# Ranks read as marked minima, and a third target one-hot of eight on ScalarE, in a graph convolution on one core

## The chip, the cores and the metric

One Trainium2 chip, one of its cores. The metric is the device time of one execution of the program in microseconds (us). The kernel before takes 6993.59 us, the median of 3 runs (6985.06 to 7000.94).

## What is computed

Two graph convolutions over 25,000 nodes and 250,000 edges, then a lookup of 102,400 rows. Cut to what matters:

```python
def gcn_conv(x, W, b, row, col, num_nodes):
    h = x @ W
    row_sl, col_sl = [row, loop], [col, loop]          # every node also has an edge to itself
    deg = segment_sum(ones, col_sl); dinv = rsqrt(max(deg, 1))
    msg = h[row_sl] * (dinv[row_sl] * dinv[col_sl])[:, None]
    return segment_sum(msg, col_sl) + b
h1 = gcn_conv(emb, W1, b1, row, col, 25000)            # 64 -> 128 features
lookup = gcn_conv(h1, W2, b2, row, col, 25000)         # 128 -> 64 features
return lookup[r_input]                                 # 512 x 200 rows of 64
```

The kernel multiplies the two weight matrices first, so both rounds of messages carry 64 features.

## The kernel before

**Stages.** (1) A histogram of the targets' blocks and degrees. (2) A counting sort of the edges by target block of 256 nodes (98 blocks), in 5 chunks of 50,000 edges; a chunk is 50 *sort batches* of 8 columns of 125 edges. (3) Round 1 of the messages: for each chunk, GpSimd gathers the source rows from a table in HBM (`L371`, 392 indirect DMAs of 128 rows per chunk, 1960 per round), and *visits* add them up: a visit makes a one-hot of the targets (128x256), multiplies it on TensorE with the 128 gathered rows (`L656`), and VectorE adds the product to the block's accumulator (`L1037`). A chunk has 61 *visit batches* of 8 visits. (4) Round 2 does the 5 chunks' visits again on the rescaled table. (5) GpSimd fetches the asked rows with 800 indirect DMAs (`L404`) and SyncE writes them out.

**The sort batch.** For batch `s`, VectorE makes block one-hots (`block_onehots`, 125x784: 8 edge columns by 98 blocks). TensorE adds to the running ranks in PSUM (`rank_ps`, 98 ranks for each of 8 columns) how many edges of lower partitions go to each block (`rank_before`, 2 matmuls of 392 columns with the triangle `before`). Then VectorE reads each edge's rank: `pick_ranks` (`L988`) multiplies ranks by one-hots, `sum_ranks` (`L994`) sums over the blocks. `rank_rest` on TensorE (2 matmuls with `not_before`) adds the rest of the batch's counts, once `pick_ranks` has read. `cut_places` splits the rank into a partition and a column, `cast_places` and `partition_onehots` turn the partition into one-hots, and `column_onehot` (`L1016`, 8 per batch, 125x488) makes the column one-hots. ScalarE scales the partition one-hots by two digits of the edge (`scale_column`, `L457`, 16 per batch), and TensorE places them (`place_column`, 16 matmuls of 488 columns).

**How the stages lie over each other.** Chunk 0 is sorted first, together with the multiplication of the embeddings by the weights (`sort_batch`, batches 0 to 48 with 4 embedding matmuls `L709` and VectorE's scaling `L1124` inside). After chunk 0's `decode` the gathers start, 6 more sort batches run (`AHEAD`), and then `both` runs one sort batch of the next chunk beside one visit batch of this one: 50 such batches for chunks 0 to 2, 44 for chunk 3, whose other 11 or 17 visit batches run alone. Chunk 4 of round 1 and all of round 2 have no sort beside them. VectorE's instructions in `both` are in the order of the list `BOTH`; TensorE's in the order of its own `both`: `rank_before(s + 1)`, then for each `k` visit `k` and column `k`, with `rank_rest(s + 1)` after `k == 0`.

**Who makes the target one-hots.** In chunks 0 to 3 of round 1, `ON_ACT = (3, 6)` names the two of eight that ScalarE makes, each by two activations (`L464`, the distance, and `L468`, one minus it); VectorE makes the other six (`L1027`). In `both`, ScalarE makes one before its 16 scalings and the other after the fourth column's. From chunk 4 of round 1 on VectorE makes all eight.

**The gathers' ring.** Gathered rows lie in a ring of 16 gather batches of 8. A gather batch may start once the visit batch is multiplied that could still use its place:

```python
if c * GB + b >= RINGB:
    c0, b0 = divmod(c * GB + b - RINGB, GB)
    done = (r * CHUNKS + c0) * VB + min(b0 + LAG, VB - 1) + 1
    pool.wait_ge(visits_multiplied, done * W8 + VISIT_CREDIT)
```

With `GB` = 49 gather batches, `VB` = 61 visit batches and `LAG` = 13, gather batch 16 of a chunk waits for visit batch 13 of the same chunk, and batches 0 to 15 for visit batches 46 to 60 of the chunk before. The gathers of a chunk also wait for its `sources_ready`, which `copy_tiles` raises during the chunk before. TensorE waits for landed rows in `wait_landed`, behind `rank_before` and ahead of the batch's first visit.

## Time and profile before

| what | value |
|---|---|
| median of 3 runs | 6993.59 us |
| the profiled execution: its own time, its span | 6975.57 us, 6973.8 us |
| granted clock of TensorE, mean | 0.692 |
| busy of the span: PE, DVE, ACT, POOL | 72%, 61%, 30%, 65% |
| gathers of both rounds (L371) | 3920, busy 3785.5 us |
| fetches of the asked rows (L404) | 800, busy 754.7 us |

The profiled execution is 18 us below the median of the runs. Busy shares are means over stages with different limits, so the stages have to be read apart; "idle before, releaser" says what an engine's idle time ended with. In the rows, PE is TensorE's matmul, PEld its weight load, DVE VectorE, ACT ScalarE, POOL GpSimd.

### The profile page before, as it was taken

Reading aid. Unit: us, or ns where it says so; the run is one execution under the profiler, and the core shown is the slowest. Engines: PE = TensorE matmul, PEld = TensorE weight load, DVE = VectorE, ACT = ScalarE, POOL = GpSimd, SP = SyncE. Lnnn points to the kernel's source line nnn. Section 1 sums busy time; section 2 is a strip of 40 time slices with the busy share of each in tenths; the row PEclk is TensorE's granted clock in tenths of the full one; section 3 lists DMA queues with packets and bytes.
Section 4 is the critical chain, followed back from the end, with each engine's and each line's share of the span. In section 5 each row is a group of like instructions: output and inputs, shape, how many; then the busy total and the mean of one; then the engine's idle time right before and its main releaser. Section 6 shows DMA issues by size and latency. Waiting matters only on the chain.

```text
span 6973.8 us, 133704 instructions
## 1 busy us (share of the span) xinstructions
PE 5035.2 (72%) x27034; PEld 4251.7 (61%) x27035; DVE 4284.9 (61%) x14137; ACT 2098.6 (30%) x6145; POOL 4543.0 (65%) x4733
## 2 busy tenths in 40 slices
PE   6858788888888888899788888888888888100000
PEld 5633355755655665799788888888888888100000
DVE  8988899899889889767566555555555555000000
ACT  7957666566566566511100000000000011000000
POOL 0000377767767767777677777777777777677777
PEclk9989999899899999855555555555555555555555
DMA  0001111111111111111111111111111111111111
GB/s 14 0 18 39 27 25 25 27 21 25 26 21 25 26 20 25 26 36 41 37 26 26 26 26 26 26 26 26 26 26 26 34 39 39 45 53 53 53 53 52
DMA packets 184476, 210.96 MB, mean 30 GB/s; under 512 B 81356, under 2 KB 100182, under 8 KB 184336
## 3 DMA queue, kind: packets, MB, share of 16 engines
q0 software_dynamic: 151040, 154.97, 11.3%
q1 hardware_dynamic: 15280, 35.45, 1.3%
q10 hardware_dynamic: 18016, 19.05, 0.9%
q8 instruction: 42, 0.69, 0.0%
q14 instruction: 98, 0.80, 0.0%
HBM read 163.62 MB, written 45.54 MB: 30 GB/s over the span
## 4 chain that ended last, share of the span: by engine, by line
PE 34%; POOL 25%; issue 19%; DVE 14%; DMA 6%; DVEq 3%; ACT 0%; POOLq 0%; SPq 0%; ACTq 0%
PE ps L656 24%; POOL scratch L371 14%; POOL acc L404 11%; PE ps L561 9%; DMA scratch<-table,source 5%; DVE late L1016 3%; DVE place_i L994 3%; DVE acc L1037 2%; DVE hi_onehot L829 2%; DVE late L1027 1%; DVE picked L988 1%; PE ps L709 1%; DVE prt_onehot L829 0%; DVEq L1035 0%; DVEq L1027 0%
## 5 line engine op out<-in xcount | busy, mean ns | idle before, releaser
L371 POOL DMA_INDIRECT scratch<-table,source x3920 | 3785.5, 966 | 2154.1 <-issue 1104.5
L656 PEld LDWEIGHTS ps<-scratch,late 128*128 128x128 f32 x19520 | 3685.6, 283 | 766.2 <-issue 643.7
L656 PE MATMUL ps<-scratch,late 128*128 x19520 | 3723.5, 368 | 455.6 <-SPq L336 259.6
L1037 DVE TENSOR_TENSOR acc<-acc,ps 128x128 f32 x4880 | 1357.8, 278 | 1250.9 <-PE ps L656 1225.9
L1027 DVE TENSOR_SCALAR late<-ramp,target 128x256 f32<-128x256 f16 x4392 | 1654.2, 377 | 162.1 <-issue 95.0
L457 ACT ACTIVATE late<-prt_onehot,scratch 125x128 f16<-125x128 f16 x4000 | 1214.7, 387 | 699.6 <-DVE prt_onehot L829 600.0
L561 PE MATMUL ps<-late 125*128 125x488 f16 x4000 | 1125.1, 372 | 164.6 <-DVE late L1016 164.5
L404 POOL DMA_INDIRECT acc<-lookup,scratch x800 | 754.7, 943 | 267.4 <-issue 243.5
L533 ACT ACTIVATE acc<-acc,dinv (+1 forms) x196 | 57.5, 340 | 2441.9 <-DVE acc L1037 2441.9
L1016 DVE TENSOR_SCALAR late<-ramp,tcol 125x488 f16<-125x488 f16 x2000 | 685.0, 350 | 0.0
L561 PEld LDWEIGHTS ps<-late 125*128 125x128 f16 x4000 | 363.7, 113 | 314.7 <-DVE late L1016 203.7
L561 PE MATMUL ps<-scratch,hi_onehot 125*98 125x265 f16 x2000 | 283.2, 283 | 67.8 <-DVE hi_onehot L829 51.3
L438 ACT ACTIVATE scratch<-ramp,acc 125x257 f16<-125x257 f16 x750 | 317.7, 501 | 27.1 <-DVE scratch L838 16.3
L468 ACT ACTIVATE late<-distance,one_col 128x256 f32<-128x256 f16 x488 | 247.8, 508 | 258.1 <-PE ps L656 216.5
L988 DVE TENSOR_TENSOR picked<-ps,blk_onehot 125x784 f32<-125x784 f32 x250 | 243.6, 975 | 132.9 <-PE ps L561 132.1
L561 PEld LDWEIGHTS ps<-scratch,hi_onehot 125*98 125x98 f16 x2000 | 215.8, 125 | 135.3 <-DVE hi_onehot L829 131.0
L464 ACT ACTIVATE distance<-ramp,target 128x256 f16<-128x256 f16 x488 | 241.8, 496 | 3.6
L994 DVE TENSOR_REDUCE place_i<-picked 125x8 int32<-125x784 f32 x250 | 239.5, 958 | 0.0
L829 DVE TENSOR_TENSOR scratch<-ramp,acc 125x1280 f16<-125x1280 f16 x250 | 206.0, 824 | 17.9 <-PE ps L561 5.1
L533 ACT ACTIVATE acc<-acc,dtmp (+1 forms) x196 | 57.5, 340 | 407.5 <-DVE acc L1037 407.5
L561 PE MATMUL ps<-blk_onehot,not_before 125*128 125x392 f16 x500 | 128.0, 338 | 71.3 <-DVE picked L988 67.1
L561 PE MATMUL ps<-blk_onehot,before 125*128 125x392 f16 x500 | 126.8, 336 | 64.0 <-issue 53.7
(145 smaller groups left out, 1079.1 us busy)
## 6 DMA issues: line engine op xcount, KB each, us to landing
scratch<-table,source POOLq DMA_INDIRECT x3920, 2.5
out<-acc SPq DMA_DIRECT2D x40, 640.0 KB, 3.0
acc<-lookup,scratch POOLq DMA_INDIRECT x800, 2.4
table<-acc SPq DMA_DIRECT2D x49, 128.0 KB, 2.5
table<-acc ACTq DMA_DIRECT2D x49, 128.0 KB
lookup<-acc ACTq DMA_DIRECT2D x49, 128.0 KB
late<-embT ACTq DMA_DIRECT2D x47, 128.0 KB, 2.7
scratch<-edge_index SPq DMA_DIRECT2D x2, 976.6 KB
```

The costliest lines, as they stand in the source:

```text
L371: pool.indirect_dma_start(out=place, out_offset=None, in_=table[r], in_offset=bass.IndirectOffsetOnAxis(ap=source[:, t:t + 1], axis=0)).th ...
L404: pool.indirect_dma_start(out=out_rows[:, h, k, :], out_offset=None, in_=lookup, in_offset=bass.IndirectOffsetOnAxis(ap=ask_i[:, t:t + 1], ...
L438: act.activation(lo_rows[0:EP, b, j, 0:LOW + 1], ramp[0:EP, 0:LOW + 1], ACT.Sign, bias=lo_half[0:EP, bass.ds((i * 2 + b) * W8 + (c * CB * ...
L457: act.activation(piece[0:EP, k, j, :], prt_onehot[0:EP, b, j, :], ACT.Copy, scale=digit[k][0:EP, bass.ds(s * W8 + j, 1)]).then_inc(pieces_ ...
L561: return pe.matmul(dst, lhsT, rhs, start=False, stop=False, skip_group_check=True)
L656: last = pe.matmul(visit_ps[odd * W8 + k][:, n * FEAT:(n + 1) * FEAT], target_onehot[:, odd * W8 + k, n * P:(n + 1) * P], row, start=True, ...
L829: return dve.tensor_tensor(place.rearrange("p j (w r) -> p j w r", r=2), of_row.rearrange("p (w r) -> p w r", r=2).unsqueeze(1).broadcast_ ...
L988: dve.tensor_tensor(picked[E, :, :].rearrange("p (h j) n -> p h (j n)", h=2), rank_ps[E, :, :], blk_onehot[E, :, :].rearrange("p (h j) n - ...
L994: dve.tensor_reduce(place_i[E, 0, :], picked[E, :, :], AX.X, ALU.add).then_inc(rank_step, 1)
L1016: dve.tensor_scalar(tcol_onehot[E, j % TRING, :], ramp[E, 0:CV], tcol[E, b, j:j + 1], None, ALU.is_equal).then_inc(tcol_onehots, 1)
L1027: dve.tensor_scalar(target_onehot[:, odd * W8 + k, :], ramp[:, 0:BN], target[:, bass.ds((g - r * BATCHES) * W8 + k, 1)], None, ALU.is_equa ...
L1037: dve.tensor_tensor(dst, dst, visit_ps[odd * W8 + k].rearrange("p (n f) -> p n f", f=FEAT), ALU.add).then_inc(visits_added, 1)
```

## The change

`pick_ranks` and `sum_ranks` become one instruction, `least_ranks`. The triangle `before` carries -65536 on its diagonal, so after `rank_before` the rank of the block that an edge goes to is by far the least of its 98, and a minimum over the blocks, read straight from PSUM, gives it. The mark is a multiple of 128 and 512, so cutting out partition and column drops it. `rank_rest` takes it away again: `after` carries +65536 on the diagonal, and a second matrix, `itself`, adds the edge's own 1, so `rank_rest` is 4 matmuls, not 2. The matrices and the block one-hots are BF16. `rank_rest` stands later in TensorE's order (after column 1 in the sort alone, after column 2 in `both`). ScalarE makes the one-hots 2, 5 and 7. GpSimd makes three more small matrices at the start.

```diff
-ON_ACT = (3, 6)
+ON_ACT = (2, 5, 7)
...
-        blk_onehot = sb("blk_onehot", [P, W8, NB], F16)
-        picked = sb("picked", [P, W8, NB], F32)
+        blk_onehot = sb("blk_onehot", [P, W8, NB], BF16)
...
-            pool.affine_select(out=not_before[:, :], in_=ones[:, :], compare_op=ALU.is_ge, fill=0.0,
+            pool.affine_select(out=after[:, :], in_=ones[:, :], compare_op=ALU.is_gt, fill=0.0,
                                base=0, pattern=[[-1, P]], channel_multiplier=1).then_inc(triangles_made, 1)
+            pool.affine_select(out=itself[:, :], in_=ones[:, :], compare_op=ALU.is_equal, fill=0.0,
+                               base=0, pattern=[[1, P]], channel_multiplier=-1).then_inc(triangles_made, 1)
+            pool.wait_ge(triangles_made, 3)
+            for triangle, mark in ((before, -MARK), (after, MARK)):
+                pool.affine_select(out=triangle[:, :], in_=triangle[:, :], compare_op=ALU.not_equal, fill=float(mark),
+                                   base=0, pattern=[[1, P]], channel_multiplier=-1).then_inc(triangles_made, 1)
...
                     scale_column(s, j, b)
-                    if j == 3 and between is not None:
-                        act_onehot(between, ON_ACT[1], odd)
+                    if between is not None and j in (2, 5):
+                        act_onehot(between, ON_ACT[1 + j // 5], odd)
...
                 pe.wait_ge(rank_step, s * RANK + 1)
-                for h in range(2):
-                    last = add(rank_ps[:, h, :], not_before[0:EP, :], halves[0:EP, h, :])
+                for counted_by in (after, itself):
+                    for h in range(2):
+                        last = add(rank_ps[:, h, :], counted_by[0:EP, :], halves[0:EP, h, :])
                 last.then_inc(rank_advanced, 1)
...
                 place_column(s, 0)
+                place_column(s, 1)
                 rank_rest(s + 1)
-                place_column(s, 1)
                 pe.wait_ge(emb_loaded[b], i * 16 + 16)
...
-                    if more and k == 0:
+                    if more and k == 2:
                         rank_rest(s + 1)
...
-            def pick_ranks(s):
+            def least_ranks(s):
+
                 dve.wait_ge(rank_summed, s + 1)
-                dve.tensor_tensor(picked[E, :, :].rearrange("p (h j) n -> p h (j n)", h=2), rank_ps[E, :, :],
-                                  blk_onehot[E, :, :].rearrange("p (h j) n -> p h (j n)", h=2), ALU.mult).then_inc(rank_step, 1)
-
-            def sum_ranks(s):
-                dve.wait_ge(rank_step, s * RANK + 1)
-                with nc.allow_low_precision(reason="one whole number among zeros"):
-                    dve.tensor_reduce(place_i[E, 0, :], picked[E, :, :], AX.X,
-                                      ALU.add).then_inc(rank_step, 1)
+                with nc.allow_low_precision(reason="a whole number"):
+                    dve.tensor_reduce(place_i[E, 0, :].rearrange("p (h j) -> p h j", h=2),
+                                      rank_ps[E, :, :].rearrange("p h (j n) -> p h j n", n=NB), AX.X,
+                                      ALU.min).then_inc(rank_step, 1)
...
-BOTH = [("blocks",), ("target", 0), ("column", 0), ("late add", 4), ("target", 1), ("pick",), ("late add", 5), ("column", 1),
-        ("target", 2), ("sum",), ("late add", 6), ("column", 2), ("cut",), ("late add", 7), ("column", 3), ("load",),
-        ("target", 4), ("add", 0), ("cast",), ("column", 4), ("target", 5), ("add", 1), ("partitions",), ("column", 5),
-        ("add", 2), ("column", 6), ("target", 7), ("add", 3), ("column", 7)]
+BOTH = [("blocks",), ("target", 0), ("column", 0), ("late add", 4), ("target", 1), ("late add", 5), ("column", 1),
+        ("target", 3), ("least",), ("late add", 6), ("column", 2), ("cut",), ("late add", 7), ("column", 3), ("load",),
+        ("target", 4), ("add", 0), ("cast",), ("column", 4), ("target", 6), ("add", 1), ("partitions",), ("column", 5),
+        ("add", 2), ("column", 6), ("add", 3), ("column", 7)]
```

How the order moves, at the places that the prediction speaks of. First VectorE in `both`, the first half of a batch, from the block one-hots on (`tcol` are the column one-hots, `target` the target one-hots, `picked` and the reduction the two steps of reading the ranks; the adds are not in the part of the loop shown, whose first batch has none). Before:

```order
L829 TENSOR_TENSOR blk_onehot<-ramp,scratch 125x784
L1027 TENSOR_SCALAR late<-ramp,target 128x256
L1016 TENSOR_SCALAR late<-ramp,tcol 125x488
L1027 TENSOR_SCALAR late<-ramp,target 128x256
L988 TENSOR_TENSOR picked<-ps,blk_onehot 125x784
L1016 TENSOR_SCALAR late<-ramp,tcol 125x488
L1027 TENSOR_SCALAR late<-ramp,target 128x256
L994 TENSOR_REDUCE place_i<-picked 125x8
L1016 TENSOR_SCALAR late<-ramp,tcol 125x488
L1000 TENSOR_SCALAR place_i<-place_i 125x8
```

Of the change:

```order
L840 TENSOR_TENSOR blk_onehot<-ramp,scratch 125x784
L1036 TENSOR_SCALAR late<-ramp,target 128x256
L1025 TENSOR_SCALAR late<-ramp,tcol 125x488
L1036 TENSOR_SCALAR late<-ramp,target 128x256
L1025 TENSOR_SCALAR late<-ramp,tcol 125x488
L1036 TENSOR_SCALAR late<-ramp,target 128x256
L1001 TENSOR_REDUCE place_i<-ps 125x8
L1025 TENSOR_SCALAR late<-ramp,tcol 125x488
L1008 TENSOR_SCALAR place_i<-place_i 125x8
L1009 TENSOR_SCALAR tcol<-place_i 125x8
```

`L988` is gone, the reduction (now `L1001`) reads `ps`, and it stands one column and one target one-hot later behind the block one-hots.

TensorE in `sort_batch`, from `rank_before` to the embedding matmuls (`late` are the pieces that are placed; `L618` and `L628` hold the wait for the ranks' reading). Before:

```order
L561 MATMUL ps<-blk_onehot,before 128x392 x2
L624 ISA
L625 ISA
L561 MATMUL ps<-late 128x488 x2
L618 ISA
L561 MATMUL ps<-blk_onehot,not_before 128x392 x2
L624 REGISTER_ALU
L625 REGISTER_ALU
L561 MATMUL ps<-late 128x488 x2
L709 MATMUL ps<-w,late 128x64 x4
```

Of the change:

```order
L571 MATMUL ps<-blk_onehot,before 128x392 x2
L635 ISA
L636 ISA
L571 MATMUL ps<-late 128x488 x2
L635 REGISTER_ALU
L636 REGISTER_ALU
L571 MATMUL ps<-late 128x488 x2
L628 ISA
L571 MATMUL ps<-blk_onehot,after 128x392 x2
L571 MATMUL ps<-blk_onehot,itself 128x392 x2
L720 MATMUL ps<-w,late 128x64 x4
```

Column 1's two matmuls moved ahead of the wait, and behind it stand four rank matmuls, directly ahead of the embedding matmuls.

TensorE in `both`, around `rank_rest` (`scratch,late` is a visit). Before:

```order
L656 MATMUL ps<-scratch,late 128x64 x2
L624 ISA
L625 ISA
L561 MATMUL ps<-late 128x488 x2
L618 ISA
L561 MATMUL ps<-blk_onehot,not_before 128x392 x2
L649 REGISTER_ALU
L653 ISA
L656 MATMUL ps<-scratch,late 128x64 x2
```

Of the change:

```order
L667 MATMUL ps<-scratch,late 128x64 x2
L635 REGISTER_ALU
L636 REGISTER_ALU
L571 MATMUL ps<-late 128x488 x2
L628 ISA
L571 MATMUL ps<-blk_onehot,after 128x392 x2
L571 MATMUL ps<-blk_onehot,itself 128x392 x2
L660 REGISTER_ALU
L664 ISA
L667 MATMUL ps<-scratch,late 128x64 x2
```

`rank_rest` now follows the third column and not the first, and has four matmuls.

## Rows read from the trace of the kernel before

**Rows 1.** The page: POOL's busy share and TensorE's granted clock in 40 slices.

```profile
POOL 0000377767767767777677777777777777677777
PEclk9989999899899999855555555555555555555555
```

**Rows 2.** Busy time by stretch: stretch, length, PE, PEld, DVE, ACT, POOL, clock, DMA.

```profile
1513.00:2058.00 545.00, 469.79 (x2960) 335.78 (x2960) 483.21 (x1615) 351.84 (x1044) 390.57 (x391) 0.96 0.13 24
...
3104.00:3440.00 336.00, 310.76 (x1447) 308.93 (x1447) 223.19 (x863) 42.26 (x144) 251.87 (x266) 0.50 0.18 40
3466.00:5950.00 2484.00, 2106.67 (x9715) 2082.32 (x9715) 1351.63 (x5061) 55.16 (x188) 1853.99 (x1960) 0.50 0.15 28
5967.00:6973.00 1006.00, 0.00 (x0) 0.00 (x0) 0.00 (x0) 0.00 (x0) 754.73 (x800) 0.50 0.16 52
```

**Rows 3.** Waits from 831 to 2990 us (us, times, longest), and one in POOL's timeline.

```profile
POOL scratch L371 <- PE ps L656: 118.7, 75, 34.2
...
1505.78 0.94 POOL L371 DMA_INDIRECT scratch<-table,source  x1 [30.11 <-PE ps L656]
```

**Rows 4.** Timeline of DVE, one batch of both: start, us, what, idle before.

```profile
1609.72 0.55 DVE L829 TENSOR_TENSOR blk_onehot<-ramp,scratch 125x784 f16<-125x784 f16 x1
1610.20 0.34 DVE L1027 TENSOR_SCALAR late<-ramp,target 128x256 f32<-128x256 f16 x1
1610.46 0.34 DVE L1016 TENSOR_SCALAR late<-ramp,tcol 125x488 f16<-125x488 f16 x1
...
1611.47 0.97 DVE L988 TENSOR_TENSOR picked<-ps,blk_onehot 125x784 f32<-125x784 f32 x1 [0.21 <-PE ps L561]
1612.36 0.28 DVE L1037 TENSOR_TENSOR acc<-acc,ps 128x128 f32 x1
...
1613.15 0.95 DVE L994 TENSOR_REDUCE place_i<-picked 125x8 int32<-125x784 f32 x1
...
1619.17 0.55 DVE L829 TENSOR_TENSOR blk_onehot<-ramp,scratch 125x784 f16<-125x784 f16 x1
```

**Rows 5.** Timeline of PE in the same batch: ranks, visits, a column, visits.

```profile
1612.50 0.51 PE L561 MATMUL ps<-blk_onehot,not_before 125*128 125x392 f16 x2 [0.17 <-DVE picked L988]
1612.84 0.56 PE L656 MATMUL ps<-scratch,late 128*128 x4
1613.24 0.58 PE L561 MATMUL ps<-late 125*128 125x488 f16 x2
1613.65 0.55 PE L656 MATMUL ps<-scratch,late 128*128 x4
```

**Rows 6.** Timeline of ACT in the same batch.

```profile
1611.75 2.43 ACT L457 ACTIVATE late<-prt_onehot,scratch 125x128 f16<-125x128 f16 x8
1614.09 0.50 ACT L464 ACTIVATE distance<-ramp,target 128x256 f16<-128x256 f16 x1
1614.70 0.51 ACT L468 ACTIVATE late<-distance,one_col 128x256 f32<-128x256 f16 x1
1617.83 1.57 ACT L457 ACTIVATE late<-prt_onehot,scratch 125x128 f16<-125x128 f16 x5 [2.62 <-DVE prt_onehot L829]
```

**Rows 7.** Timeline of PE, then of DVE, in one batch of the sort alone.

```profile
611.80 0.51 PE L561 MATMUL ps<-blk_onehot,not_before 125*128 125x392 f16 x2 [0.66 <-DVE picked L988]
...
607.24 0.42 DVE L1124 TENSOR_TENSOR acc<-ps,dinv 128x256 f32 x1 [0.32 <-PE ps L709]
...
610.77 0.97 DVE L988 TENSOR_TENSOR picked<-ps,blk_onehot 125x784 f32<-125x784 f32 x1 [0.75 <-PE ps L561]
...
613.93 0.42 DVE L1124 TENSOR_TENSOR acc<-ps,dinv 128x256 f32 x1 [0.32 <-PE ps L709]
```

**Rows 8.** Timeline of POOL: a gather beside DVE's partition one-hots (1607.48 to 1608.16).

```profile
1607.56 1.42 POOL L371 DMA_INDIRECT scratch<-table,source  x1 [0.30 <-issue]
```

**Rows 9.** A stretch at the granted clock of 0.50, and a column pair in it.

```profile
434.00:442.00 8.00, 4.25 (x11) 1.06 (x12) 5.95 (x13) 2.52 (x9) 0.00 (x0) 0.50 0.08 5
...
440.61 1.02 PE L561 MATMUL ps<-late 125*128 125x488 f16 x2
```

More of the change, by code:

```diff
@@ L120, in build @@
         ones = sb("ones", [P, P], F16)
-        before = sb("before", [P, P], F16)
-        not_before = sb("not_before", [P, P], F16)
+        before = sb("before", [P, P], BF16)
+        after = sb("after", [P, P], BF16)
+        itself = sb("itself", [P, P], BF16)
         hi_onehot = sb("hi_onehot", [P, 2, W8, NT], F16)
@@ L1101, in first_places @@
                 block_onehots(s)
-                pick_ranks(s)
-                sum_ranks(s)
+                least_ranks(s)
                 cut_places(s, 0)
@@ L1168, in both @@
                         block_onehots(s + 1)
-                    elif what == "pick":
-                        pick_ranks(s + 1)
-                    elif what == "sum":
-                        sum_ranks(s + 1)
+                    elif what == "least":
+                        least_ranks(s + 1)
                     elif what == "cut":
```

29 lines of the change are left out of this document (15 added, 14 removed).

## The prediction, made before the changed kernel was run

> **What bounds the kernel now.** I read the page's 40 slices first [rows 1]: POOL has the same seven or eight tenths in nearly every slice from 793 us to the end, while PE, DVE and ACT change from stage to stage. So the gathers may set the end, and the question for each stage is whether POOL works back to back. The table of stretches answers it [rows 2]. In round 2 1960 gathers take 2484 us, 1.267 us each. In the last 266 gathers of round 1 they come every 336 / 266 = 1.263 us. The same pace in both: POOL is the bound there, with PE at the lower clock level (0.50 granted) and still not in the way. The fetches of the asked rows, 800 in 1006 us, are also one after another. Nothing of the change touches these stages.
>
> In chunks 1 to 3 of round 1, where sort and visits run together, POOL makes 391 gathers in 545 us, 1.394 us each [rows 2]. Its waits show why: 118.7 us of them end with a visit on TensorE. Most of the 75 are the usual 0.3 us between two gathers, but once per chunk, in chunks 1 to 3, POOL stands still for 30 to 34 us [rows 3]. This is the ring's wait of gather batch 16 for visit batch 13 of the same chunk. Without it the chunk's gathers would take 545 - 31 = 514 us (1.315 us each, a little over round 2's pace). So the period of a chunk is set by the sort and visit batches, but **only by 31 us**; behind them stands POOL.
>
> What sets those batches is VectorE. From one block one-hot to the next it takes 1619.17 - 1609.72 = 9.45 us [rows 4], and idles only 0.21 us ahead of `pick_ranks` and shortly at the register load. ScalarE waits 2.62 us for the partition one-hots [rows 6].
>
> Before the gathers there are 49 sort batches with embeddings, 613.93 - 607.24 = 6.69 us each [rows 7].
>
> **The change, part by part.**
>
> *The first gather.* It starts when chunk 0 is sorted, so the sort alone is on the path, and a reading by busy time would promise 49 x 0.97 us for the lost `pick_ranks`. The timeline says otherwise [rows 7]: VectorE's embedding scaling waits 0.32 us for TensorE's embedding matmuls, and these stand behind `rank_rest`, which waits for `pick_ranks` to end. The new minimum starts where `pick_ranks` started (behind `rank_before`, which VectorE already awaits for 0.75 us, time enough for one more column one-hot), so if it lasts as long, `rank_rest` is released at the same moment. It then has two matmuls more, and one column pair fewer ahead of the embedding matmuls. A rank pair costs 1612.84 - 1612.50 = 0.34 us, a column pair 1613.65 - 1613.24 = 0.41 us [rows 5]. The batch gets 0.41 - 0.34 = 0.07 us shorter, and VectorE waits about 1.2 us for the embedding matmuls instead of 0.32. That is 49 x 0.07 = 3.4 us, say **-4 us** with the one batch without embeddings. The minimum's duration is unknown: nearest are the reduction over as many elements from SBUF (0.95 us) and the product that reads the same ranks from PSUM (0.97 us) [rows 4]. I take 0.97; a reduction that costs the two together, 1.92, is the other end, and one at half the product's time, 0.5, the lower.
>
> *A batch of `both` on VectorE.* Gone are `pick_ranks` with its slot, 1612.36 - 1611.47 = 0.89 us, the wait ahead of it, 0.21 us, which two more instructions now cover, and one target one-hot, 1610.46 - 1610.20 = 0.26 us [rows 4]. 9.45 - 1.36 = **8.1 us**.
>
> *The same batch on TensorE.* At the full clock a visit and a column pair take 1613.65 - 1612.84 = 0.81 us [rows 5]. 8 x 0.81 + 2 rank matmuls before and now 4 after, 3 x 0.34 = 1.0 us, makes 7.5 us, under 8.1. In its new place `rank_rest` finds the minimum done, because column 2, ahead of it, is made behind the minimum on VectorE.
>
> *The same batch on ScalarE.* 8 scalings take 1614.09 - 1611.75 = 2.34 us, a one-hot's first step 0.61 us and its second 0.51 at most. 2 x 2.34 + 3 x 1.12 = 8.0 us [rows 6], also under 8.1, but near: three engines now lie within 0.6 us. The third one-hot's 1.12 us is hidden in the 2.62 us that ScalarE waits; where that cover is gone it is on the path. I allow 8.4 us for the batch in all.
>
> *The chunk.* 50 batches that are 9.45 - 8.4 = 1.05 us or more shorter bring the chunk's own work from 545 to 492 us or less. POOL needs 514. So the ring's wait vanishes, POOL works without a pause, TensorE waits instead for landed rows, and **the period becomes POOL's 514 us**. The gain is the waits and no more: 118.7 less 75 x 0.3 = **-96 us** [rows 3]. It stands for any batch under 9.45 - 31 / 50 = 8.83 us: most of what the change saves on VectorE (50 x 1.36 = 68 us a chunk) lands in a wait.
>
> *At no cost:* three more small matrices on GpSimd, which has no other work before the first gather at 793 us; BF16 for F16, two bytes either way; the mask in `cut_places`, inside an instruction that is there anyway.
>
> *Sum:* -4 - 96 = -100 us. The profiled execution took 6975.6 us, so 6875.6 by its measure; the median of the runs is 18 us above it, so **6893.6 us**. A measurement of this kernel tells 0.2%, 14 us, from no change.
>
> **The rivals.**
>
> *The batch shrinks too little* (chance 0.15). The minimum costs the two old steps together, or the three near-equal engines wait for each other. At 9.1 us a batch the chunk's work is 545 - 17.5 = 527 us, the ring's wait is still 13 us of 31, and three chunks give some 55 us with the start's gain: 6939 us. For it: VectorE, TensorE and ScalarE at 8.1, 7.5 and 8.0. Against it: the bound to clear is 8.83.
>
> *The gathers slow down* (0.05). A gather beside the partition one-hots took 1.42 instead of 0.94 us [rows 8]. If a denser VectorE meets one such in every batch where now it meets fewer, up to 50 x 0.48 = 24 us a chunk are added to 514, and the end is within 20 us of today's, 6985 us. Against it: the number of these instructions per gather does not grow.
>
> *The clock falls* (0.05, the slower side). TensorE gets a new wait inside `both`, for landed rows, ahead of each batch's first visit. The granted clock in chunks 1 to 3 is now 0.96, that is mostly the 2.4 GHz level; in the visits without a sort beside them it is 0.50, 1.2 GHz, with PE 85% to 92% busy [rows 2]. If the waits bring the lower level into `both`, columns cost 0.82 us a pair instead of 0.41 (1.02 us for a pair from first start to last end, against 0.58) and ranks double likewise [rows 5, 9]; a visit costs at most 336 us / 1447 x 4 = 0.93 us, against 0.40 [rows 2, 5]. The batch is then 8 x 1.75 + 2 = 16 us, 7.6 us over the 8.4 allowed. The decisive point is (545 - 492) / 7.6 = 7 batches of 50: beyond it a chunk is longer than today. With one in four, 12, it is 492 + 91 = 583 us, 38 more than today for each of four chunks: 7145 us, or some 7070 us if the lone visits catch up half of it. Against it: a batch of 8.4 to 8.8 us holds the same matmuls as one of 9.45, so PE is denser, not thinner. The Trainium skill (TensorE: Matmul & The Clock Gate, The HAM clock gate) says that recent activity releases the throttle and that waits inside the loop bring it back; by that rule the new wait would argue for this rival, while the denser batch argues against.
>
> *More is gained* (0.09). Either the sort alone does shorten by VectorE's 0.97 us, 49 x 0.97 = 48 us instead of 4, or POOL's pace in `both` comes down to round 2's 1.267 us, 391 x 0.048 = 19 us a chunk: 6820 to 6850 us. The Trainium skill (SBUF — State Buffer, Who interferes with whom) says that GpSimd shares a port pair with VectorE, that `tensor_scalar` in its faster modes takes the pair for its whole duration and that `tensor_reduce` never does; by that rule a target one-hot fewer on VectorE helps the gathers. One of 14 such instructions in a batch is worth 19 / 14 = 1.4 us a chunk by the rows, so I leave it out of the sum.
>
> *The batch does not shrink at all*, because ScalarE's late one-hots hold TensorE (0.02): 6990 us.
>
> **How the numbers follow.** The forecast has 0.64. With the first rival and the larger gain, faster by over 0.2% has 0.64 + 0.15 + 0.09 = 0.88; the slower gathers and the batch that doesn't shrink make 0.07 for within 0.2%; the clock makes 0.05 for slower. The range runs from 6855, the forecast with a part of the larger gain, to 6950, the first rival with 10 us of scatter of the runs. It leaves out the three cases at the top and most of the larger gain.
>
> **What would show it.** Right: the three waits of 30 us on POOL are gone, and 391 gathers take 510 to 520 us; the wait of PE for SyncE's count of landings, which in round 1's chunks does not occur now, appears; blocks of one-hots come every 8.1 to 8.8 us; VectorE's wait for the embedding matmuls grows to about 1.2 us while the batch stays near 6.6 us; the first gather starts 3 to 6 us earlier; the reduction from PSUM takes about 0.97 us. Wrong: waits of POOL for visits that remain (the batch is over 8.83 us), a granted clock well under 0.95 in chunks 1 to 3, or a first gather tens of us earlier.

## The result, and the profile after

The changed kernel takes **6868.89 us** (6868.16 to 6871.3, 4 runs), the kernel before in the same comparison 6996.85 us (6985.06 to 7000.94, 4 runs): ratio 0.982, 95% interval 0.9803 to 0.9837. That is 128 us less; the forecast was 100 less, 6893.6 us. The profiled executions took 6975.57 and 6869.0 us, 106.6 us apart.

The page of the changed kernel, busy time and the slices of POOL and of TensorE's granted clock, against [rows 1]:

```profile
span 6867.3 us, 134775 instructions
PE 5034.4 (73%) x27534; PEld 4382.0 (64%) x27535; DVE 4014.0 (58%) x13643; ACT 2327.5 (34%) x6633; POOL 4539.2 (66%) x4736
...
POOL 0000377777777777777677777777777777677777
PEclk9989999899899899555555555555555555555555
```

POOL's sixes in slices 9, 12 and 15, the starts of chunks 1 to 3, are gone; the two left, slices 20 and 35, are the steps from round 1 to round 2 and from round 2 to the fetches, and stand in the kernel before too.

Busy time by stretch of the changed kernel, columns as in [rows 2]: chunk 2, the last 272 gathers of round 1, round 2, the fetches:

```profile
1447.00:1960.00 513.00, 472.06 (x3077) 374.77 (x3076) 426.73 (x1513) 409.32 (x1169) 386.99 (x392) 0.90 0.13 26
2990.00:3333.00 343.00, 292.75 (x1351) 289.27 (x1351) 206.55 (x801) 39.91 (x136) 257.01 (x272) 0.50 0.18 39
3360.00:5843.00 2483.00, 2106.56 (x9714) 2082.23 (x9714) 1349.76 (x5061) 55.15 (x188) 1854.11 (x1960) 0.50 0.15 28
5860.00:6867.00 1007.00, 0.00 (x0) 0.00 (x0) 0.00 (x0) 0.00 (x0) 755.05 (x800) 0.50 0.17 52
```

Only the first row has changed: 392 gathers in 513 us, where 391 took 545. ScalarE's busy time there rose from 352 to 409 us, VectorE's fell from 483 to 427. The clock fell from 0.96 to 0.90.

Waits of the changed kernel from 700 to 2900 us (total, times, longest), against [rows 3], and at the end POOL's own row from 700 to 3500 us (in a row, `a <- b` is a waiting for b):

```profile
DVE acc L1046 <- PE ps L667: 133.8, 70, 5.7
ACT late L467 <- DVE prt_onehot L840: 100.5, 87, 15.3
...
PE ps L667 <- SPq L340: 72.9, 33, 4.2
...
POOL scratch L381 <- PE ps L667: 23.5, 77, 0.3
```

POOL's waits for a visit are down to 77 of 0.3 us; the three of 30 us are gone. New is TensorE's wait for SyncE's count of landings, 72.9 us in 33 pieces: TensorE is now ahead of the rows.

VectorE and TensorE in the sort alone, one batch of the changed kernel, against [rows 7]:

```profile
606.83 0.97 DVE L1001 TENSOR_REDUCE place_i<-ps 125x8 int32<-125x784 f32 x1 [0.49 <-PE ps L571]
...
607.87 0.51 PE L571 MATMUL ps<-blk_onehot,after 125*128 125x392 bf16 x2 [0.25 <-DVE place_i L1001]
...
608.21 0.49 PE L571 MATMUL ps<-blk_onehot,itself 125*128 125x392 bf16 x2
...
608.63 1.10 PE L720 MATMUL ps<-w,late 64*128 64x64 f32 x8
...
609.92 0.42 DVE L1131 TENSOR_TENSOR acc<-ps,dinv 128x256 f32 x1 [1.38 <-PE ps L720]
...
613.45 0.97 DVE L1001 TENSOR_REDUCE place_i<-ps 125x8 int32<-125x784 f32 x1 [0.48 <-PE ps L571]
```

The minimum from PSUM takes 0.97 us. The batch takes 613.45 - 606.83 = 6.62 us, where it took 6.69: what VectorE saved now stands in its wait for the embedding matmuls, 1.38 us instead of 0.32.

**Where the 106 us of the trace come from.** POOL's time up to the last gather of round 1 can be closed as a sum: start of the first gather, plus what its waits for a visit exceed the usual 0.3 us each ("excess"), plus what the 1960 gathers last beyond 0.944 us each ("lengthening"; 0.944 us is their median), plus a rest. For every kernel of the table the rest is 2471 to 2475 us, so these three columns explain the difference between any two to within 4 us. (Added up from the records of each trace, one execution each, us; the kernels below the second are the experiments. The medians come from three groups of runs, so they compare to some 13 us: the kernel before had 6996.9, 6984.9 and 6983.7 in the three.)

| kernel | first gather | excess | lengthening | last gather of round 1 | median of runs |
|---|---|---|---|---|---|
| before | 793.2 | 96.2 | 81.2 | 3442.7 | 6996.9 |
| changed | 786.6 | 0.4 | 76.1 | 3336.4 | 6868.9 |
| ranks alone | 787.8 | 0.3 | 112.6 | 3371.6 | 6901.0 |
| third one-hot alone | 794.2 | 69.1 | 72.9 | 3408.0 | 6960.2 |
| changed + two minima | 788.0 | 166.4 | 53.4 | 3482.4 | 7031.7 |
| changed + a one-hot | 787.6 | 0.4 | 58.6 | 3317.8 | 6849.0 |
| changed + a short minimum | 788.1 | 0.3 | 56.0 | 3317.2 | 6845.2 |
| changed, embedding first | 734.5 | 0.4 | 77.0 | 3283.7 | 6815.9 |
| before, embedding first | 789.1 | 112.0 | 77.8 | 3451.1 | 6986.1 |

From before to changed: -6.6, -95.8, -5.1, and 1.2 in the rest. Nine tenths of the gain are the waits.

### The profile page after: what moved, and what is told of

The parts are those of the page before. It is cut to its first block, busy times and chain, and to the rows that moved or that the text cites. A ratio compares the mean times of both kernels' runs of the same rounds, so it can differ in the third digit from the quotient of the medians.

```text
span 6867.3 us, 134775 instructions
## 1 busy us (share of the span) xinstructions
PE 5034.4 (73%) x27534; PEld 4382.0 (64%) x27535; DVE 4014.0 (58%) x13643; ACT 2327.5 (34%) x6633; POOL 4539.2 (66%) x4736
## 4 chain that ended last, share of the span: by engine, by line
PE 36%; POOL 30%; issue 17%; DVE 7%; DMA 7%; DVEq 2%; ACT 0%; POOLq 0%; SPq 0%; ACTq 0%
PE ps L667 25%; POOL scratch L381 19%; POOL acc L414 11%; PE ps L571 10%; DMA scratch<-table,source 7%; DVE hi_onehot L840 2%; DVE acc L1046 1%; DVE place_i L1001 1%; DVE late L1025 1%; PE ps L720 1%; DVE late L1036 1%; DVE scratch L840 0%; DVEq L1044 0%; DVEq L854 0%; DVE prt_onehot L840 0%
## 5 line engine op out<-in xcount | busy, mean ns | idle before, releaser
L667 PEld LDWEIGHTS ps<-scratch,late 128*128 128x128 f32 x19520 | 3751.6, 286 | 822.4 <-issue 657.5
L1036 DVE TENSOR_SCALAR late<-ramp,target 128x256 f32<-128x256 f16 x4148 | 1564.2, 377 | 149.0 <-issue 71.5
L467 ACT ACTIVATE late<-prt_onehot,scratch 125x128 f16<-125x128 f16 x4000 | 1236.4, 387 | 306.3 <-DVE prt_onehot L840 151.2
L571 PEld LDWEIGHTS ps<-late 125*128 125x128 f16 x4000 | 397.6, 119 | 146.2 <-DVE late L1025 60.8
L478 ACT ACTIVATE late<-distance,one_col 128x256 f32<-128x256 f16 x732 | 371.8, 508 | 263.9 <-PE ps L667 199.6
L474 ACT ACTIVATE distance<-ramp,target 128x256 f16<-128x256 f16 x732 | 362.9, 496 | 5.2
L448 ACT ACTIVATE scratch<-ramp,acc 125x257 f16<-125x257 f16 x750 | 318.5, 501 | 26.4 <-DVE scratch L849 16.3
L1001 DVE TENSOR_REDUCE place_i<-ps 125x8 int32<-125x784 f32 x250 | 241.6, 967 | 67.5 <-PE ps L571 67.2
L840 DVE TENSOR_TENSOR prt_onehot<-ramp,prt 125x1024 f16<-125x1024 f16 x250 | 170.1, 681 | 0.3
L840 DVE TENSOR_TENSOR blk_onehot<-ramp,scratch 125x784 bf16<-125x784 f16 x250 | 140.0, 560 | 10.3 <-issue 9.8
L571 PE MATMUL ps<-blk_onehot,before 125*128 125x392 bf16 x500 | 126.6, 335 | 25.1 <-issue 19.0
```

Of the source, the lines that this page charges most:

```text
L448: act.activation(lo_rows[0:EP, b, j, 0:LOW + 1], ramp[0:EP, 0:LOW + 1], ACT.Sign, bias=lo_half[0:EP, bass.ds((i * 2 + b) * W8 + (c * CB * ...
L467: act.activation(piece[0:EP, k, j, :], prt_onehot[0:EP, b, j, :], ACT.Copy, scale=digit[k][0:EP, bass.ds(s * W8 + j, 1)]).then_inc(pieces_ ...
L474: act.activation(distance[:, 0:BN], ramp[:, 0:BN], ACT.Abs, bias=target[:, bass.ds(g * W8 + k, 1)], scale=-1.0).then_inc(distances, 1)
L478: act.activation(target_onehot[:, odd * W8 + k, :], distance[:, 0:BN], ACT.Relu, bias=one_col[:, 0:1], scale=-1.0).then_inc(act_onehots, 1)
L571: return pe.matmul(dst, lhsT, rhs, start=False, stop=False, skip_group_check=True)
L667: last = pe.matmul(visit_ps[odd * W8 + k][:, n * FEAT:(n + 1) * FEAT], target_onehot[:, odd * W8 + k, n * P:(n + 1) * P], row, start=True, ...
```

## Experiments

My theory: POOL's own pace is a floor of 514 us a chunk, VectorE's batch sets the time only above 8.83 us, and in the sort alone the order on TensorE, not VectorE's work, sets the batch. The rivals: each us of VectorE counts wherever it is; it was ScalarE's one-hots or the clock; POOL's pace itself changes. (The *knee* below is the 8.83 us at which, by the prediction, VectorE's batch takes over from POOL.)

### First group: four kernels on a chip that behaves otherwise

*Ranks alone*: the changed kernel with two of eight on ScalarE again. *Third alone*: the kernel before, with three.

```diff
 # ranks alone, against the changed kernel
-ON_ACT = (2, 5, 7)
+ON_ACT = (3, 6)
 # third alone, against the kernel before: the same line the other way
```

(The conditions at ScalarE's columns and the target entries of the `BOTH` table follow it.) *Least twice* and *least thrice*: one or two spare minima into an unused tile, in every batch of `both`:

```diff
                 dve.wait_ge(rank_summed, s + 1)
+                for k in range(again):
...
+                        dve.tensor_reduce(spare_i[E, k, :]..., rank_ps[E, :, :]..., AX.X, ALU.min)
```

> The marked minimum without the third one-hot on ScalarE. Theory (round 1's chunks end with GpSimd's 514 us once a batch of both is under 8.83 us): VectorE's batch is 8.1 + 0.26 = 8.4 us, still under 8.83, so no wait of POOL for a visit over 1 us, and the time is the changed kernel's within 0.2%, 6869 us plus or minus 14. Rival (each part gives its share of VectorE's time, 1.1 and 0.26 us of 1.36): a fifth of the 106 us is missing, 6890 us.

> The kernel before with ScalarE making one-hots 2, 5 and 7. Theory: VectorE's batch is 9.45 - 0.26 = 9.2 us, over 8.83, so the long waits of POOL stay but shrink by 50 x 0.26 = 13 us each to some 18 us; three of them give 40 us, about 6955 us; the first gather stays at 793 us. Rival (ScalarE is in the way): no change, 6997 us.

> The changed kernel, with a second minimum of the same ranks, into a spare tile, in each batch of both. Theory: a batch is 8.1 + 0.89 = 9.0 us, just over the knee of 8.83; a chunk's own work is 545 - 50 x 0.47 = 521 us against POOL's 514, so waits of about 7 us are back once per chunk and the time is some 20 us above the changed kernel's, 6890 us. Rival (VectorE bounds round 1): 194 x 0.89 = 173 us slower, 7040 us.

> As before it with two spare minima in each batch of both. Theory: a batch is 9.9 us, past the knee each further microsecond counts: 50 x 0.89 = 44 us per chunk over the run with one spare minimum, in the three waits 134 us more, about 7025 us, and POOL waits of some 50 us. Rival (slack is left elsewhere): under 60 us more than the run with one spare minimum.

Measured: 9192.61, 9270.21, 9200.81 and 9243.82 us, where the kernel before took **9261.68 us** (9229 to 9283, 19 runs) on this chip. Ratios 0.9927 [0.9906, 0.9948], 1.0011 [1.0002, 1.0021], 0.9933 [0.9911, 0.9955], 0.9984 [0.9971, 0.9996]. The changed kernel itself was not run there. None of the expectations could be judged: another bound stood over them. The third one-hot alone ran later on an ordinary chip too, so one kernel's stretches (the sort alone, a chunk of `both`, round 2) can be set side by side. On this chip:

```profile
440.00:740.00 300.00, 244.47 (x1237) 119.27 (x1238) 250.23 (x709) 214.81 (x716) 0.00 (x0) 0.98 0.14 39
1878.00:2651.00 773.00, 550.69 (x2971) 409.67 (x2970) 475.65 (x1561) 412.82 (x1167) 387.47 (x392) 0.80 0.09 17
4680.00:8050.00 3370.00, 2133.01 (x9307) 2034.13 (x9308) 1337.57 (x4845) 42.84 (x146) 1851.53 (x1957) 0.50 0.11 20
```

and on the ordinary one:

```profile
440.00:740.00 300.00, 244.51 (x1236) 119.34 (x1236) 250.24 (x709) 214.63 (x715) 0.00 (x0) 0.98 0.14 39
2022.00:2568.00 546.00, 476.61 (x2972) 347.95 (x2970) 476.08 (x1562) 408.50 (x1167) 387.45 (x392) 0.94 0.14 24
3432.00:5905.00 2473.00, 2102.34 (x9695) 2078.18 (x9696) 1345.94 (x5053) 55.16 (x188) 1850.54 (x1959) 0.50 0.16 28
```

The sort alone is the same to 0.2 us of busy time, and the busy times of POOL and VectorE agree to 1% in the other two. What differs is idle time once gathers run: 3370 us for what takes 2473. VectorE's waits in 500 us of round 2 there:

```profile
DVE acc L1037 <- issue: 104.7, 79, 3.9
DVE late L1027 <- issue: 86.6, 66, 4.1
```

These are stretches of up to 4 us for which the profile shows no releaser ("issue" takes 9.7 us in a like stretch on the ordinary chip). The cause is open. The profiles of these four kernels give no time from issue to landing for any gather (the ordinary ones give a median of 2.5 us), so a late landing may hide behind "issue"; the expectation of the ranks alone below takes the landings for the bound, which no run shows. What follows is only that there the change's two parts lie under a slower regime: the ranks' new form gave 0.7%, the third one-hot nothing.

### Second group: the two parts, the knee, and the order on TensorE

Here the kernel before took 6984.85 us (6969.15 to 6994.32, 11 runs). The first three repeat kernels of the first group; the one with a single spare minimum, whose 9.0 us would lie just past the knee, was not run again.

**Ranks alone.**

> The changed kernel with two target one-hots on ScalarE again, so that the marked minima stand alone; now, if the kernel before takes about 6997 us on this chip. My theory: a batch of both parts takes 9.45 less 0.89 (products) less 0.21 (wait) = 8.35 us, under the 8.83 us at which POOL's gathers take over, so round 1 has no ring waits and the time is that of the whole change, 6869 +- 14 us. Rival (the gain is VectorE's time, batch by batch): 0.26 us of 200 batches short of the whole change's gain, some 6920 us. If the kernel before takes about 9262 us here as in the first runs, the landing of the gathered tiles is the bound and it gives 0.993 as before.

Measured: 6901.02 us (6898.6 to 6904.2), ratio 0.9884 [0.9867, 0.99]. Between both numbers, and neither theory's way of getting there: POOL waits for no visit longer than its usual 0.3 us, and yet is slower. POOL alone from the 521st to the 1696th gather, three chunks' worth (stretch, length, busy and count, clock, DMA):

```profile
1484.40:3038.60 1554.20, 1181.34 (x1176) 0.84 0.15 26
```

and the same of the changed kernel:

```profile
1472.60:3004.00 1531.40, 1155.84 (x1177) 0.84 0.14 27
```

The instruction itself lasts longer, 1.005 us on average instead of 0.982. Two partition one-hots of the ranks alone, with what runs on both engines around them, show how:

```profile
1886.83 1.05 POOL L381 DMA_INDIRECT scratch<-table,source  x1 [0.30 <-issue]
...
1887.59 0.42 DVE L1036 TENSOR_SCALAR late<-ramp,target 128x256 f32<-128x256 f16 x1
...
1887.92 0.27 DVE L1046 TENSOR_TENSOR acc<-acc,ps 128x128 f32 x1
...
1888.12 0.68 DVE L840 TENSOR_TENSOR prt_onehot<-ramp,prt 125x1024 f16<-125x1024 f16 x1
...
1888.19 1.42 POOL L381 DMA_INDIRECT scratch<-table,source  x1 [0.30 <-issue]
...
1889.91 0.95 POOL L381 DMA_INDIRECT scratch<-table,source  x1 [0.30 <-issue]
...
1896.31 0.68 DVE L840 TENSOR_TENSOR prt_onehot<-ramp,prt 125x1024 f16<-125x1024 f16 x1
1896.39 1.42 POOL L381 DMA_INDIRECT scratch<-table,source  x1 [0.30 <-DMA scratch<-table,source]
```

They began 0.07 and 0.08 us before a gather, and that gather lasted 1.42 us. I sorted all 125 partition one-hots of this stretch by when they began after the last gather's start. Those that began 1.15 to 1.35 us after it, just ahead of the next one, lengthened that next one by 0.48 us: 73 of 74 in the ranks alone, 48 of 50 in the changed kernel. Those that began in the first 0.65 us of a gather never lengthened it by more than 0.15 us.

That so many fall at this one moment is no chance. Every partition one-hot of round 1 that began 0.07 to 0.08 us ahead of a gather (118 in the ranks alone, 88 in the changed kernel) began 0.22 to 0.23 us after the end of the gather before it, as at 1888.12. The rows show the way there once: the target one-hot at 1887.59 takes 0.42 us where its like takes 0.35, ends behind the gather of 1886.83, and the add and the partition one-hot follow it back to back.

**The third one-hot alone.**

> The kernel before, its ranks unchanged, with the third target one-hot on ScalarE alone; if the kernel before takes about 6997 us here. My theory: the batch of both parts goes from 9.45 to about 9.19 us, still above the 8.83 us, so round 1's waits shrink by 0.26 x 50 = 13 us a chunk in three chunks, and stay: waits of about 18 us at each chunk's start, time about 6957 us. Rival (ScalarE's one-hots were what stood in the way): no waits left and about 6900 us. Second rival: ScalarE becomes late with its columns, no gain. If the kernel before takes about 9262 us: 1.001 as before.

Measured: 6960.21 us (6939.24 to 6973.06, 8 runs), ratio 0.9965 [0.9949, 0.9981]. That is my theory's number to 3 us, but by luck: it was reckoned from 6997 us, and the kernel before took 6984.85 here, so the gain is 25 us where 40 were expected. The batch shrank by 0.13 us, to 9.32, and not by 0.26. What stands is the theory's kind of result: waits that remain and are shorter. "No waits, 6900 us" and "no gain" are both excluded. POOL's waits for a visit from 700 to 3500 us:

```profile
POOL scratch L371 <- PE ps L656: 97.6, 95, 33.8
```

The three at the starts of chunks are 20.5, 15.2 and 33.8 us. Batches take 9.32 us at the median, so the knee gives (9.32 - 8.83) x 50 = 24.5 us; their mean is 23.2, but the last did not shrink at all (34.2 before). The stretches that end with the second and the third wait, and 41 us inside the latter:

```profile
1494.00:2023.00 529.00, 457.06 (x2975) 327.01 (x2974) 477.35 (x1564) 409.13 (x1169) 388.92 (x393) 0.99 0.14 25
2023.00:2568.00 545.00, 475.84 (x2968) 347.63 (x2967) 475.43 (x1559) 407.61 (x1165) 387.04 (x392) 0.94 0.14 24
...
2400.00:2441.00 41.00, 41.00 (x193) 40.09 (x193) 22.41 (x80) 19.79 (x47) 31.25 (x33) 0.51 0.16 27
```

VectorE and POOL are as busy in both; TensorE is busy 19 us longer for the same matmuls at a mean granted clock of 0.94 instead of 0.99, and the wait is 19 us longer. By this trace the length of the wait above the knee depends on TensorE's clock too: the 41 us, at 1.2 GHz, lie in the visits without a sort beside them that every chunk has.

**Two spare minima.**

> The changed kernel with two spare minima (0.97 us each) in each batch of both parts, so that a batch takes some 8.1 + 1.9 to 2.0 = 10.1 us on VectorE; if the kernel before takes about 6997 us here. My theory of a knee at 8.83 us: the last 1.3 us of it are above the knee, so 1.3 x 50 = 65 us of wait at each start of chunks 1 to 3 and more inside them, beyond before's 31; round 1's end some 3 x 62 us later than before's less what chunk 4 gives back: about 7050 us, within 7000 to 7110. Rival (no knee, each us of VectorE counts): 6869 + 200 x 1.95 = 7259 us. If the kernel before takes about 9262 us: 0.998 as before.

Measured: 7031.68 us (7013.68 to 7038.33), ratio 1.0075 [1.0058, 1.0092]. No-knee is excluded by 227 us. The batches take 9.78 to 9.89 us, so a minimum costs a slot of (9.85 - 8.1) / 2 = 0.87 us and not 0.97, and the knee gives (9.85 - 8.83) x 50 = 51 us a chunk. The three waits are 59.6, 51.7 and 53.1:

```profile
POOL scratch L382 <- PE ps L668: 196.1, 99, 59.6
```

Above the knee the model is right to 10% for the mean of the three waits in both kernels. Where the knee lies is shown only between 8.4 us (no waits, below) and 9.3 us.

**Embedding first.** TensorE's embedding matmuls in `sort_batch` before the ranks' second part:

```diff
                 place_column(s, 1)
-                rank_rest(s + 1)
                 pe.wait_ge(emb_loaded[b], i * 16 + 16)
...
                 last.then_inc(emb_multiplied, 1)
+                rank_rest(s + 1)
                 for j in range(2, W8):
```

> The changed kernel with PE's two embedding matmuls ahead of the ranks' second part in the batch that sorts alone. VectorE waits 1.37 us there for them in each of 49 batches, while PE does eight matmuls of the ranks and the wait for halves first. My theory: that wait is what took the saved products' time; with it gone a batch takes 5.6 to 5.9 us instead of 6.6, the first gather starts 35 to 48 us earlier (at about 745 us) and the time falls by as much, since POOL's gathers are the bound from there on: about 6828 us if the kernel before takes about 6997 us here. Rival: the ranks' second part is then late for the minimum, the wait only moves from L1131 to L1001, and nothing changes (6869). If the kernel before takes about 9262 us here: 35 to 48 us less than the changed kernel in either regime, since this stage has no gathers.

Measured: **6815.88 us** (6814.89 to 6820.14), ratio 0.9765 [0.9748, 0.9781], the fastest of all: 169 us under the kernel before. The first gather starts at 734.5 us, 52.1 earlier, and the whole time falls by 53.0, a little more than the 35 to 48 us expected; 2.7 us of it lie ahead of the first sort batch, which the edit doesn't touch. In the trace the wait is down from 1.38 to 0.29 us, and TensorE is what is full: busy 291 of 300 us. The sort alone, then one batch in it:

```profile
440.00:740.00 300.00, 291.38 (x1532) 154.51 (x1532) 251.48 (x779) 245.23 (x816) 4.31 (x5) 0.97 0.15 42
...
602.68 0.97 DVE L1001 TENSOR_REDUCE place_i<-ps 125x8 int32<-125x784 f32 x1 [0.49 <-PE ps L571]
...
604.69 0.42 DVE L1131 TENSOR_TENSOR acc<-ps,dinv 128x256 f32 x1 [0.29 <-PE ps L719]
```

The changed kernel has TensorE busy 262.41 us in the same 300. The batch takes 5.53 us at the median instead of 6.62.

### Third group: what lengthens a gather, and what the order gives by itself

The kernel before took 6983.69 us (6956.55 to 7002.59, 15 runs). Ahead of the minimum of `both`, one more instruction of about the same length that goes nowhere, in one kernel a one-hot from SBUF, in the other a read of PSUM:

```diff
 # spare one-hot
+                    dve.tensor_scalar(spare_f[:, :], ramp[:, 0:BN], target[:, 0:1], None, ALU.is_equal)
 # spare minimum
...
+                        dve.tensor_reduce(spare_i[E, 0:3], rank_ps[E, 0, 0:3 * NB]..., AX.X, ALU.min)
```

> The changed kernel with one spare target one-hot (tensor_scalar, fp16 from SBUF, about 0.26 to 0.34 us) on VectorE in each batch of both parts, ahead of the minimum: VectorE's batch goes from about 8.1 to 8.4 us, as with the ranks alone (8.3), with nothing changed on ScalarE. Theory 1 (formed from the ranks alone, 6901 us, where POOL never waited for PE and its gathers in round 1 were longer by 36 us in sum): a gather that meets a one-hot on VectorE is held up, so POOL's own pace depends on how many there are and how they fall; 6885 to 6905 us, with POOL's lengthening in round 1 at 95 to 115 us instead of 76. Theory 2 (as I predicted: POOL's own pace is fixed, and a batch under 8.83 us costs nothing): 6869 us. Theory 3 (only the length of the batch counts): 6885 to 6905 us as well, and the spare minimum of the next run gives the same. If the kernel before takes about 9262 us here, another bound hides all this.

> The same place and about the same duration, but the spare instruction is a minimum over three blocks of ranks in PSUM (tensor_reduce, about 0.35 us). Theory 1 (one-hots from SBUF hold POOL up, a read of PSUM does not): about 6869 us, and at most 6880, with POOL's lengthening in round 1 at about 76 us. Theory 2 (fixed pace, batch under 8.83): 6869 us too. Theory 3 (only the length of VectorE's batch counts): the same as the spare one-hot, 6885 to 6905 us.

Measured: 6849.0 us (6847.75 to 6857.98), ratio 0.9808 [0.9791, 0.9826], and 6845.23 us (6844.82 to 6857.79), ratio 0.9804 [0.9786, 0.9821]. **All three theories fall.** More work on VectorE, batches of 8.3 to 8.4 us instead of 8.1, and neither kernel is slower than the changed one; by the runs they are 20 us faster, though that compares different groups, and the intervals of the ratios overlap. The traces are sharper: the last gather of round 1 starts 19 us earlier, with a lengthening that is 18 and 20 us less. The short minimum's POOL in the same 1176 gathers, and two of its partition one-hots:

```profile
1463.30:2983.80 1520.50, 1146.03 (x1176) 0.86 0.15 27
...
1879.84 1.05 POOL L382 DMA_INDIRECT scratch<-table,source  x1 [0.31 <-DMA scratch<-table,source]
...
1880.18 0.69 DVE L841 TENSOR_TENSOR prt_onehot<-ramp,prt 125x1024 f16<-125x1024 f16 x1
...
1881.19 0.94 POOL L382 DMA_INDIRECT scratch<-table,source  x1 [0.30 <-PE ps L668]
...
1888.43 0.68 DVE L841 TENSOR_TENSOR prt_onehot<-ramp,prt 125x1024 f16<-125x1024 f16 x1
1888.85 1.10 POOL L382 DMA_INDIRECT scratch<-table,source  x1 [0.30 <-issue]
```

Here they begin 0.34 us into a gather, or 0.42 us before one, and cost it 0.11 and 0.16 us. Only 7 of 125 began just ahead of a gather (21 with the spare one-hot, 48 and 73 above).

The partition one-hots are not all of it. I added up the lengthening of round 1's gathers by the instruction that VectorE had under way when each gather began (us, from the records):

| VectorE at the gather's start | before | ranks alone | changed | + a one-hot | + a short minimum |
|---|---|---|---|---|---|
| partition one-hots | 31.7 | 59.3 | 44.0 | 29.0 | 17.6 |
| column one-hots | 21.2 | 27.8 | 5.8 | 2.4 | 2.1 |
| target one-hots | 10.3 | 16.9 | 12.3 | 6.3 | 13.7 |
| block one-hots | 16.3 | 7.5 | 12.5 | 16.8 | 18.7 |
| all | 81.2 | 112.6 | 76.1 | 58.6 | 56.0 |

From before to the ranks alone the partition one-hots make 28 of the 31 us more. From there to the changed kernel they make 15 of the 36 us less, and the column one-hots 22. ("All" has the few gathers beside anything else too.) The ranks alone and the spare one-hot have the same number of VectorE's instructions in a batch and batches of 8.3 and 8.3 to 8.4 us, and their lengthening is 112.6 and 58.6 us. So it is neither the number of instructions nor the batch's length, but **where VectorE's one-hots fall between POOL's gathers**. That is read from the records; no kernel moved the one-hots and nothing else, and I could not say beforehand in which kernel they fall well.

The Trainium skill (SBUF — State Buffer, Who interferes with whom) says that a VectorE instruction with two inputs in SBUF contends with a GpSimd instruction that reads SBUF, and that the order of issue decides who blocks. The trace agrees for the one-hot that begins first, a `tensor_tensor` with both inputs in SBUF, where the gather's indices, `source`, lie too: 1.42 us for 0.94. Where the gather begins first the one-hot takes the same 0.68 to 0.69 us. The same section infers that a `tensor_tensor` does not hold up the writing of descriptors; which part of the gather's 1.42 us is held up, reading or writing, no run here shows.

**The order without the new ranks.** The edit of "embedding first" on the kernel before:

> The kernel before, with PE's two embedding matmuls ahead of the ranks' second part in the sort alone; the same edit took 52 us from the changed kernel (first gather 786.6 to 734.5 us). Theory: in the kernel before VectorE waits only 0.3 us there, so at most 0.3 us x 49 = 15 us of first gather are to be had, and none if the products and the sum then wait for the ranks' second part instead: first gather 778 to 794 us, time 6970 to 6985 us if the kernel before takes about 6985 us. So the ranks' new form saves the sort alone some 40 to 50 us once the order of PE lets it. Rival: the order alone is worth 52 us in either kernel: first gather at 741 us, about 6930 us.

Measured: 6986.12 us (6970.98 to 6994.01, 10 runs), ratio 1.0005 [0.9991, 1.0018]: no difference, as expected; the first gather starts 4 us earlier. The order alone is worth nothing in the time, on the new ranks it is worth 53 us. That is where `pick_ranks`' 0.97 us in each of 49 batches was.

**Scaling late.** "Embedding first", and VectorE's `acc` scaling in `sort_batch` moved behind the last column one-hot:

```diff
                 partition_onehots(s + 1, 1 - b)
                 for j in range(4, W8):
                     column_onehot(s, j, b)
+                if emb:
+                    ...
```

> The changed kernel with the embedding matmuls first on PE, and VectorE's embedding scaling moved behind columns 4 to 7 in the sort alone. Theory: with the matmuls first 0.3 us of VectorE's wait is left (14.6 us in 45 batches), so the scaling's new place is worth at most 15 us: first gather 720 to 735 us, time 6800 to 6816 us. Rival: the next batch's late scaling holds the block one-hots or ScalarE's load of the next embedding: first gather later than 735 us.

Measured: 6816.56 us (6813.84 to 6818.19), ratio 0.9761 [0.974, 0.9782]; first gather at 733.6 us. The edge of what I expected, and no gain over 6815.88. TensorE was busy in 291 of 300 us already; that this is the reason is argued, not shown.

## Why the prediction was right, and where not

**The ring's waits, -96.** Right in size and place: the excess went from 96.2 to 0.4 us. The batch is 8.1 to 8.2 us (medians of four stretches) for 8.1, a chunk 513 us for 514. Two spare minima and the third one-hot alone show from above that waits come back with a longer batch. The batch's parts were less exact than their sum: a target one-hot less was taken at 0.26 us and took 0.13 off the kernel before and 0.1 to 0.2 off the ranks alone.

**The sort alone, -4.** Right, -6.6 (3 to 6 us had been named as its sign). The wait of VectorE for the embedding matmuls is 1.38 us for about 1.2, the batch 6.62 for 6.6, the minimum 0.97 as taken. The embedding-first pair of kernels shows that the order on TensorE held back the rest.

**The offset of the runs.** The term of the sum that was wrong is "the median of the runs is 18 us above it, so 6893.6 us". The sum by the profiled execution gave 6875.6, and 6869.0 was measured; the median of the runs lies on it. I carried the offset over as if it belonged to the measurement, and it belonged to that execution. So of the 25 us between the forecast 6893.6 and the measured 6868.9, 18 are this and 7 the trace's own difference. Kernels in which POOL waits for visits scatter (before 6956.55 to 7002.59, the third one-hot alone 6939.24 to 6973.06); those in which it never waits repeat to 3 to 6 us (changed 3, ranks alone 6, embedding first 5), except the two with a spare, 10 and 13, whose profiled execution is the slow one, 9 and 13 us above the median. The profiled execution of a waiting kernel can lie low (18, 21 and 18 us: before, third one-hot alone, two minima) or not (1.4 us: before, embedding first).

The scatter goes with TensorE's clock. Of the 15 runs of the kernel before in the third group the fastest, 6956.55 us, had a mean granted clock of 0.696 and the slowest, 7002.59 us, 0.688; of the 8 with the third one-hot alone the three at 6939 to 6941 us had 0.692 or 0.693, the four from 6964 to 6973 us 0.687 or 0.688. All four runs of the changed kernel have 0.671 or 0.672. That fits the waits above, which are longer where the clock is lower; no run sets the clock by itself, so it is not shown as the cause.

**"POOL needs 514".** Taken as a constant, and "it stands for any batch under 8.83 us" with it. In this change it held, and as a rule it is false: with no excess of waits to speak of and batches of 8.1, 8.3 and 8.3 us, the same three chunks' worth of gathers took 1531, 1554 and 1520 us (changed, ranks alone, short minimum). The rival that the gathers slow down, given 0.05 for the whole change, happened in one of its two parts: the ranks alone have 31 us more lengthening than before, 28 of them beside the partition one-hots, as its row said. The reason I gave against it, that their number per gather doesn't grow, was the wrong question. And the value that I gave a one-hot less on VectorE, 1.4 us a chunk, is not a value that it has: one removed (and two moved) took 36 us of lengthening off round 1, one added took 17 off again.

**The clock.** The mark I had set (well under 0.95) was touched: 0.90. TensorE's pairs of column matmuls in the changed kernel, behind a wait for landings:

```profile
1613.16 0.65 PE L667 MATMUL ps<-scratch,late 128*128 x4 [4.16 <-SPq L340]
...
1613.65 0.58 PE L571 MATMUL ps<-late 125*128 125x488 f16 x2
...
1614.67 1.02 PE L571 MATMUL ps<-late 125*128 125x488 f16 x2
...
1616.23 1.02 PE L571 MATMUL ps<-late 125*128 125x488 f16 x2
...
1618.39 0.58 PE L571 MATMUL ps<-late 125*128 125x488 f16 x2
```

After 4.16 us without work one pair still takes 0.58 us, the next two 1.02, the duration that belonged to a granted 0.50 in [rows 9], the 1.2 GHz level; the pair at 1618.39 is back at 0.58. What that rival feared is there, in short pieces, and round 1 pays nothing for it: TensorE is busy 472 of the chunk's 513 us, and POOL does not wait. The wait for landings is not needed for such pieces: with the two spare minima, where that wait does not occur in round 1's chunks, the chunks' mean is 0.95 and not 1 either.

**ScalarE.** Its wait for the partition one-hots covered the third one-hot, as costed: 518.8 us of that wait before (from 831 to 2990 us), 100.5 us now (from 700 to 2900 us).

## What to carry to other kernels

Count a removed wait, not the removed work: here 1.3 us of 200 batches were worth 96 us because POOL, the next bound, stood 31 us a chunk behind, and 0.97 us of 49 batches were worth nothing until an order on another engine was changed too. Once an engine is the bound back to back, look at how long its own instructions last next to a neighbour's, one by one, before and after: here their alignment was worth 17 to 37 us from one kernel to the next, of either sign, as much as the 25 us that the third one-hot gave by itself, so a gain of that size should not be credited to the edit. And do not carry the distance between the profiled execution and the median over to a kernel with another bound.

## What was not expected of the hardware

- A gather on POOL that starts 0.07 us after the start of a 0.68 us `tensor_tensor` of VectorE lasts 1.42 us; one in which the `tensor_tensor` starts after 0.34 us lasts 1.05. With what the other one-hots add, round 1's gathers were 53 to 113 us longer in sum, by kernel. The unfavourable start is a preferred one: in the ranks alone 118 of 199 partition one-hots had it.
- A chip on which the same program takes 9262 instead of about 6985 us, with nearly equal busy times of POOL and VectorE, and, in round 2, idle time of up to 4 us a time that no event in the profile explains. It begins with the gathers.
- Inside a stretch whose mean granted clock is 0.90, behind a wait of 4.16 us, TensorE's matmuls take up to twice as long for 3 to 4 us and then their old time again.
- In a kernel whose engines wait for each other, runs of the same program differ by up to 46 us, and the slower ones have the lower mean granted clock (0.688 against 0.696).
